# In the attention stage's tensor queue, three projection products stand ahead of each turn of the probabilities instead of behind it

## The chip, the cores and the metric

The kernel runs on one core of a Trainium2 chip. TensorE (PE) multiplies; VectorE (DVE) and ScalarE (ACT) read its result banks in PSUM; GpSimd (POOL) adds the mask; SyncE (SP) issues the DMAs. The metric is the device time of one launch in microseconds (us).

## The reference

Inputs: x of 8 batches x 512 tokens x 512 features, a bias of 8 x 16 x 512 x 512 numbers (134 MB), a mask, and the weights of two layers. Cut to what matters:

```
# layer 0: per batch either a dense net (gelu) or a small circuit, then a norm
x = layernorm(where(vol > 0.5, x + circuit(x), x + gelu(x@w1+b1)@w2+b2))
# layer 1
x = layernorm(x)*(1+scale) + shift
q, k, v = x@Wq+bq, x@Wk+bk, x@Wv+bv              # 16 heads of 32
scores = q@k.T/sqrt(32) + attention_bias; scores[mask] = -inf
ctx = softmax(scores) @ v
x = x + ctx@Wo + bo
x = x + gelu2(layernorm(x)@W1 + b1) @ W2 + b2
```

## The kernel before

There are three stages one after the other: the first dense net (to about 793 us), attention (about 793 to 1673 us), the second dense net. Only the order of TensorE's work in the attention stage is touched.

Attention goes batch by batch (8 of them, `b`), and a batch has 16 **slots** `m` (4 head groups x 4 blocks of 128 queries). A slot handles 4 **units** (the 4 heads of a group for one query block, `j` = 0 to 3; their running number is n). Everything is written out by hand in program order on each engine; semaphores tie the engines together, and an engine never passes a waiting instruction of its own.

TensorE's slot `m`, in its order:

- `scores` (L1643): 12 matmuls for the *next* slot's four units, into four score banks. Waits on `scored`: DVE must have read the scores before.
- `context` (L1660): probabilities times v for the *previous* slot's units. It waits on `pt_even` and `pt_odd`, the counts of turned probabilities that ACT (units 0 and 2) and DVE (units 1 and 3) have copied out of PSUM.
- four **quarters** `j`. In each, `turn_unit` (L1672) transposes the unit's 128 x 512 exponentials by four transposes into bank `turn[j % 2]` (waits: `exped`, and the copy of the unit two before, since it reuses its bank); and `beside` issues 3 of the 12 matmuls (L1587) of one 128 x 512 product. A slot has one such product, all twelve matmuls into one bank, `gen`: slots 0 to 3 the output projection of the batch before (`OUTS`), slots 4 to 7, 10, 11, 14, 15 a key or query projection (`KEYS`; the last four for the next batch), slots 8, 9, 12, 13 the next batch's values (`VALUES`). The last batch has none in slots 8 to 15; the first has one in slot 0 and none in 1 to 3.
- after a fourth slot, `over` (L1630): 4 transposes of the inverse sums. After slots 5 and 6, two `turn_x` (L1597): 4 transposes each of the next batch's input, into the banks `turn[0]` and `turn[1]`, each after the copy out of the unit that was there (`pt_even`, `pt_odd`).

Before the first product matmul of a slot, `gen_free` makes TensorE wait until the bank `gen` was emptied of the product of the slot before. After a slot of `KEYS` that takes two steps: `nat_hi_of` on ACT (L1299), then `nat_lo_of` on DVE (L1440), which raises `nat_lo`.

ACT's slot: [`over`, L1324, at phase starts], emptying of `gen` where it is ACT's (L1299, L1305), then copy of unit 0 (L1318), `exp` of the next slot's units 0 and 1 (L1311), [`context_hi`, L1330, at phase starts], copy of unit 2, `exp` of units 2 and 3.

DVE's slot: its emptying of `gen` (L1440, or L1446 after `OUTS`), bias addition and maximum of the next slot's units 0 and 1 (L1452), [`normalize`, L1473, at phase starts; `inverse` at phase ends], copy of unit 1 (L1459), L1452 of units 2 and 3, [`context_lo`, L1477, at phase starts], copy of unit 3, [mask conversion, L1431].

In slot 0 the last 3 matmuls of the output projection also wait on `ct_lo`, which `context_lo` raises:

```
            if i == 0 and steps[-1] == 3 * KT - 1:
                pe.wait_ge(ct_lo, b * PHASES + PHASES)
```

Of the kernel before, what the change touches and what calls it, by code (L numbers as in the profile page):

```python
# [1086 lines left out]
def attention_stage(nc, ctx, mem, banks, small, keep, t, scratch, ffn0, ffn1):  # L1087
# [61 lines left out]
    def following(b, m, last):  # L1149

        if m + 1 < BLOCKS:
            return b, m + 1
        return None if last else (b + 1, 0)
# [425 lines left out]
    def tensor(pe, f0, f1):  # L1579
# [10 lines left out]
        def turn_x(b, k, bank, last=False):  # L1590
            if k == 0 and last:
                pe.wait_ge(s1["affine_done"], TT)
            elif k == 0:
                pe.wait_ge(x_in, b * 32 + 16)
            for i in range(TT):
                tile = xin8[:, i, :] if last else xin[i // 2][:, i % 2, :]
                mm = pe.transpose(bank[:, i * P:(i + 1) * P], tile[:, k * P:(k + 1) * P], keep.ident[:, :])  # L1597
            mm.then_inc(x_mm, 1)

        def project(odd, tile, query, steps, bank):  # L1600
            wh, wl = weight["q" if query else "k"]
            cut = slice(tile * P, (tile + 1) * P)
            mm = part(bank[:, :], steps, lambda k: (wh[:, k, cut], wl[:, k, cut], xth[odd][:, k, :], xtl[odd][:, k, :]))
            if steps[-1] == 3 * KT - 1:
                mm.then_inc(nat_mm, 1)

        def values(odd, i, steps, bank):
            wh, wl = weight["v"]
            cut = slice(i * P, (i + 1) * P)
            mm = part(bank[:, :], steps, lambda k: (xth[odd][:, k, cut], xtl[odd][:, k, cut], wh[:, k, :], wl[:, k, :]))  # L1610
            if steps[-1] == 3 * KT - 1:
                mm.then_inc(v_mm, 1)

        def output(b, i, steps, bank):
            if i == 0 and steps[0] == 0:
                pe.wait_ge(w_lo, 4)
                pe.wait_ge(ct_lo, b * PHASES + PHASES - 1)
            if i == 0 and steps[-1] == 3 * KT - 1:
                pe.wait_ge(ct_lo, b * PHASES + PHASES)
            wh, wl = weight["o"]  # L1620
            cut = slice(i * P, (i + 1) * P)
            mm = part(bank[:, :], steps, lambda k: (cth[:, k, cut], ctl[:, k, cut], wh[:, k, :], wl[:, k, :]))
            if steps[-1] == 3 * KT - 1:
                mm.then_inc(o_mm, 1)

        def over(b, phase):
            pe.wait_ge(spread_set, b * PHASES + phase + 1)
            pe.wait_ge(pt_even, b * (UNITS // 2) + 2 * (TT * phase + TT))
            for u in range(TT):
                mm = pe.transpose(turn[0][:, u * P:(u + 1) * P], normal[:, u * P:(u + 1) * P], keep.ident[:, :])  # L1630
            mm.then_inc(over_mm, 1)

        def scores(b, m, first=False):

            tile, u = divmod(m, TT)
            if u == 0:
                pe.wait_ge(nat_lo, nat_count(b, tile, 1))
            if m or not first:
                pe.wait_ge(scored, b * UNITS + GROUP * m)
            for q, k in ((QH, KH), (QL, KH), (QH, KL)):  # L1640
                for j in range(GROUP):
                    head = nat[tile % 2][j * HD:(j + 1) * HD, :, :]
                    mm = pe.matmul(score[j][:, :], head[:, q, u * P:(u + 1) * P], head[:, k, :],  # L1643
                                   start=(q, k) == (QH, KH), stop=k == KL)
                    if k == KL:
                        mm.then_inc(score_mm, 1)

        def context(b, odd, m, first):

            tile, u = divmod(m, TT)  # L1650
            pe.wait_ge(pt_even, b * (UNITS // 2) + 2 * m + 2)
            pe.wait_ge(pt_odd, b * (UNITS // 2) + 2 * m + 2)
            if m == 0:
                pe.wait_ge(v_out, b * TT + TT)
            if u == 0 and not (first and m == 0):
                pe.wait_ge(normed, b * PHASES + tile)
            for k in range(KT):
                for j in range(GROUP):
                    h = GROUP * tile + j
                    mm = pe.matmul(ctx_ps[j * HD:(j + 1) * HD, u * P:(u + 1) * P], v[odd][:, k, h * HD:(h + 1) * HD],  # L1660
                                   pt[:, j, k, :], start=k == 0, stop=k == KT - 1)
            mm.then_inc(pv_mm, 1)

        def turn_unit(b, m, j, first):
            n = GROUP * m + j
            pe.wait_ge(exped, b * UNITS + n + 1)
            if not first or n >= 2:
                pe.wait_ge(pt_odd if n % 2 else pt_even, b * (UNITS // 2) + n // 2)
            if j == 0 and m % TT == 0 and not (first and m == 0):
                pe.wait_ge(over_out, b * PHASES + m // TT)  # L1670
            for k in range(KT):
                mm = pe.transpose(turn[n % 2][:, k * P:(k + 1) * P], bias[:, n % SLOTS, k * P:(k + 1) * P], keep.ident[:, :])  # L1672
            mm.then_inc(turned, 1)

        def gen_free(b, m, first):

            if m in OUTS and m and not first:
                pe.wait_ge(o_out, b * TT - TT + OUTS[m])
            elif m in OUTS or (m == 4 and first):
                pe.wait_ge(nat_lo, nat_count(b, 1, 0 if m == 0 and first else 1))  # L1680
            elif m == 4:
                pe.wait_ge(o_out, b * TT)
            elif m == 8:
                pe.wait_ge(nat_lo, nat_count(b, 3, 1))
            elif m in (9, 13):
                pe.wait_ge(v_out, b * TT + TT + VALUES[m])
            elif m in (10, 14):
                pe.wait_ge(v_out, b * TT + TT + VALUES[m - 1] + 1)
            elif m == 12:
                pe.wait_ge(nat_lo, nat_count(b + 1, 0, 1))  # L1690
            else:
                tile, query = KEYS[m]
                pe.wait_ge(nat_lo, nat_count(b, tile, query) - 1)

        def beside(b, odd, m, j, first, last):
            some = range(3 * j, 3 * j + 3)
            keys = FIRST_KEYS if first else KEYS
            if m in keys and (keys[m][0] < KT or not last):
                if j == 0:
                    gen_free(b, m, first)  # L1700
                tile, query = keys[m]
                project(odd if tile < KT else 1 - odd, tile % KT, query, some, gen)
            elif m in VALUES and not last:
                if j == 0:
                    gen_free(b, m, first)
                values(1 - odd, VALUES[m], some, gen)
            elif m in OUTS and not first:
                if j == 0:
                    gen_free(b, m, first)
                output(b - 1, OUTS[m], some, gen)  # L1710
            elif m in LAST_TURNS and j == 1 and last:
                if LAST_TURNS[m] == 0:
                    pe.wait_ge(nat_lo, nat_count(b, 3, 1))
                else:
                    pe.wait_ge(xt_lo, x_count(b + 1) + LAST_TURNS[m])
                turn_x(b + 1, LAST_TURNS[m], gen, True)
# [19 lines left out]
        def body(b, odd, first, last):  # L1736
            for m in range(BLOCKS):
                after = following(b, m, last)
                if after:
                    scores(*after)  # L1740
                if m:
                    context(b, odd, m - 1, first)
                elif not first:
                    context(b - 1, 1 - odd, BLOCKS - 1, False)
                for j in range(GROUP):
                    for k in TURNS.get(m - 1, ()):
                        if j == k % 2 and not last:
                            pe.wait_ge(xt_lo, x_count(b + 1) + k + 1)
                    turn_unit(b, m, j, first)
                    beside(b, odd, m, j, first, last)  # L1750
                if m % TT == TT - 1:
                    over(b, m // TT)
                for k in TURNS.get(m, ()):
                    if not last:
                        pe.wait_ge(pt_odd if k % 2 else pt_even, b * (UNITS // 2) + 2 * m + 2)
                        turn_x(b + 1, k, turn[k % 2])
# [151 lines left out]
```

## Time and profile before

| | |
|---|---|
| median of 3 runs | 2397.74 us (2396.6 to 2398.53) |
| the profiled execution's own time | 2398.12 us |
| its span, first to last instruction | 2396.3 us |
| TensorE busy | 2362.5 us (99%) |
| DVE, ACT, POOL busy | 57%, 42%, 43% |
| mean granted TensorE clock | 0.998 of full |

The span is the length of the profiled execution; the time of a run has a further 1.8 us around it. TensorE's busy time is that of pipelined matmuls, so what a slot costs is read from the starts of its instructions and not from their lengths. The attention stage is 37% of the span.

### The profile page before, as it was taken

To read this page: it belongs to the slowest core of one execution; us is meant where nothing else is said; L and a number is where in the kernel's file an instruction comes from. 1 tells how busy PE (TensorE), PEld (TensorE's weight loads), DVE (VectorE), ACT (ScalarE), POOL (GpSimd) and SP (SyncE) were. 2 spreads that over 40 slices of the span, in tenths; PEclk is the share of its full clock that TensorE was granted. 3 is DMA by queue.
4 is the path that set the end of the run, shared out by engine and by line. 5 is a ranking of instruction groups with operands and counts; after the bars stand their busy time and mean duration, and the time that the engine had idled before them with its cause. 6 is when DMAs were issued, how large, how long until landed. Compare 5 with 4: busy or idle time off the path is not lost. (4 is left out here: it accounts for less than half of the span.)

```text
span 2396.3 us, 42236 instructions
## 1 busy us (share of the span) xinstructions
PE 2362.5 (99%) x16100; PEld 1894.6 (79%) x16100; DVE 1359.5 (57%) x2749; ACT 1012.1 (42%) x2057; POOL 1019.7 (43%) x829
## 2 busy tenths in 40 slices
PE   9999999999999899999999999997999999999999
PEld 7788888888888677777777777775888888888887
DVE  7355464555557777777777777778443333323332
ACT  6132232331332776776767676767311111111111
POOL 0042341432424896767677776767113203203200
PEclk9999999999999999999999999999999999999999
DMA  7110101101122556565656566564320110110100
GB/s 231 42 45 21 44 24 55 44 18 61 44 73 102 161 182 205 168 200 163 212 158 203 170 200 194 169 211 164 123 71 1 53 53 0 53 53 1 51 35 18
DMA packets 142197, 243.94 MB, mean 102 GB/s; under 512 B 14140, under 2 KB 28620, under 8 KB 142048
## 3 DMA queue, kind: packets, MB, share of 16 engines
q1 hardware_dynamic: 141520, 241.66, 31.4%
q8 instruction: 97, 1.59, 0.3%
q14 instruction: 52, 0.43, 0.1%
q10 hardware_dynamic: 528, 0.26, 0.0%
HBM read 216.69 MB, written 25.20 MB: 101 GB/s over the span
## 5 line engine op out<-in xcount | busy, mean ns | idle before, releaser
L1254 POOL TENSOR_TENSOR at_bias<-at_bias,at_mask 128x512 f32<-128x512 f32 x512 | 596.4, 1192 | 231.7 <-DMA at_bias<-in_fside_Bx16xSxS 224.8
L646 ACT ACTIVATE L_hid<-bank,L_b1c 128x512 f32<-128x512 f32 x256 | 176.6, 690 | 962.0 <-PE bank L290 961.8
L845 DVE CAST L_hh<-L_hid 128x512 fp32r<-128x512 f32 x256 | 122.9, 480 | 739.1 <-PE bank L972 710.5
L288 PE MATMUL bank<-xth,L_w1h 128*128 128x512 f32 x1024 | 403.2, 394 | 0.1
L289 PE MATMUL bank<-xth,L_w1l 128*128 128x512 f32 x1024 | 400.0, 391 | 0.0
L290 PE MATMUL bank<-xtl,L_w1h 128*128 128x512 f32 x1024 | 399.7, 390 | 0.0
L970 PE MATMUL bank<-L_w2h,L_hh 128*128 128x512 f32 x1016 | 398.4, 392 | 0.0
L972 PE MATMUL bank<-L_w2l,L_hh 128*128 128x512 f32 x1016 | 396.0, 390 | 0.0
L971 PE MATMUL bank<-L_w2h,L_hl 128*128 128x512 f32 x1016 | 395.8, 390 | 0.0
L1311 ACT ACTIVATE at_bias<-at_bias,cos_sin 128x512 f32<-128x512 f32 x512 | 363.3, 713 | 8.5 <-DVE cos_sin L1452 8.0
L1452 DVE CUSTOM_DVE_ANT_0 at_bias<-bank,at_bias 128x512 f32<-128x512 f32 x512 | 331.3, 684 | 36.6 <-PE bank L1643 24.6
L541 POOL TENSOR_TENSOR rstd<-mv,power 128x4 f32<-128x4 f32 x24 | 25.8, 1077 | 730.1 <-DVE mv L729 730.0
L1672 PE MATMUL bank<-ident,at_bias 128*128 128x128 f32 x2048 | 313.9, 277 | 8.3 <-DVE at_pt L1459 5.5
L1672 PEld LDWEIGHTS bank<-ident,at_bias 128*128 128x128 f32 x2048 | 243.5, 141 | 84.6 <-issue 33.9
L1318 ACT ACTIVATE at_pt<-bank 128x512 f32<-128x512 f32 x256 | 152.3, 595 | 233.8 <-PE bank L1672 233.8
L847 DVE TENSOR_TENSOR L_hl<-L_hid,L_hh 128x512 fp32r<-128x512 f32 x256 | 232.4, 908 | 8.8
L1459 DVE COPY at_pt<-bank 128x512 f32<-128x512 f32 x256 | 176.0, 688 | 96.6 <-PE bank L1672 96.1
L288 PEld LDWEIGHTS bank<-xth,L_w1h 128*128 128x128 f32 x1024 | 192.6, 188 | 48.2 <-issue 8.2
L290 PEld LDWEIGHTS bank<-xtl,L_w1h 128*128 128x128 f32 x1024 | 192.7, 188 | 41.1
L289 PEld LDWEIGHTS bank<-xth,L_w1l 128*128 128x128 f32 x1024 | 192.7, 188 | 39.4
L972 PEld LDWEIGHTS bank<-L_w2l,L_hh 128*128 128x128 f32 x1016 | 190.8, 188 | 39.9
L970 PEld LDWEIGHTS bank<-L_w2h,L_hh 128*128 128x128 f32 x1016 | 190.9, 188 | 38.8
(213 smaller groups left out, 3240.9 us busy)
## 6 DMA issues: line engine op xcount, KB each, us to landing
at_bias<-in_fside_Bx16xSxS SPq DMA_DIRECT2D x256, 512.0 KB, 3.7
L_xres<-in_x SPq DMA_DIRECT2D x8, 1024.0 KB, 5.3
x_scratch<-L_xres SPq DMA_DIRECT2D x8, 1024.0 KB, 4.3
at_xres<-x_scratch SPq DMA_DIRECT2D x32, 256.0 KB, 4.3
L_xin<-x_scratch SPq DMA_DIRECT2D x8, 1024.0 KB, 5.6
L_xres<-x_scratch SPq DMA_DIRECT2D x8, 1024.0 KB, 5.6
L_ring<-in_L_cond_w SPq DMA_DIRECT2D x31, 256.0 KB, 4.9
L_xin<-in_x SPq DMA_DIRECT2D x7, 1024.0 KB, 5.2
```

Source lines behind the costliest of these rows:

```text
L288: nc_mm = pe.matmul(out, ah, bh, start=i == 0, stop=False)
L289: nc_mm = pe.matmul(out, al, bh, start=False, stop=False)
L290: nc_mm = pe.matmul(out, ah, bl, start=False, stop=i == n - 1)
L646: nc.scalar.activation(hid[m % 2][:, :], turn[m % 2][:, :], func, bias=b1c[:, m:m + 1]).then_inc(h_act, 1)
L847: nc.vector.tensor_tensor(hl[m % 2][:, :], hid[m % 2][:, :], hh[m % 2][:, :].bitcast(F32), ALU.subtract)\
L970: pe.matmul(acc[i][:, :], hh[m % 2][:, cut], w2h[:, m, :], start=m == 0, stop=False)
L971: pe.matmul(acc[i][:, :], hl[m % 2][:, cut], w2h[:, m, :], start=False, stop=False)
L972: mm = pe.matmul(acc[i][:, :], hh[m % 2][:, cut], w2l[:, m, :], start=False, stop=m == FT - 1)
L1254: nc.gpsimd.tensor_tensor(tile, tile, mask[:, m % TT, :], ALU.add).then_inc(masked, 1)
L1311: nc.scalar.activation(tile, tile, ACT.Exp, bias=neg_top[:, n % SLOTS:n % SLOTS + 1], scale=-1.0, accum_out=sums[:, n:n + 1]).then_inc(exp ...
L1452: nc.vector.tensor_tensor_reduce(bias[:, slot, :], score[j][:, :], bias[:, slot, :], -1.0, -MASKED, ALU.add, ALU.min, neg_top[:, slot:slot ...
L1672: mm = pe.transpose(turn[n % 2][:, k * P:(k + 1) * P], bias[:, n % SLOTS, k * P:(k + 1) * P], keep.ident[:, :])
```

## The change

In each quarter the call of `beside` is put ahead of the turn, and ahead of the wait on `xt_lo` that goes with it. Nothing is added or removed.

```
                 for j in range(GROUP):
+                    beside(b, odd, m, j, first, last)
                     for k in TURNS.get(m - 1, ()):
                         if j == k % 2 and not last:
                             pe.wait_ge(xt_lo, x_count(b + 1) + k + 1)
                     turn_unit(b, m, j, first)
-                    beside(b, odd, m, j, first, last)
```

The orders of DVE, ACT, POOL and SP are the same as before. What moves on TensorE is shown at three places of one middle batch. The first is TensorE at the head of slot 5 (the scores of slot 6's units, the context of slot 4's, then slot 5's first quarter), in the order before:

```order
L1643 MATMUL bank<-at_nat 128x512 x11
L1660 MATMUL bank<-at_pt,at_v 32x128 [waits at_normed,at_pt_odd,at_pt_even]
L1660 MATMUL bank<-at_pt,at_v 32x128 x15
L1672 MATMUL bank<-ident,at_bias 128x128 [waits at_pt_even,at_exped]
L1672 MATMUL bank<-ident,at_bias 128x128 x3
L1587 MATMUL bank<-xth,at_wqh 128x512 [waits at_nat_lo]
L1587 MATMUL bank<-xth,at_wql 128x512
L1587 MATMUL bank<-xtl,at_wqh 128x512
```

and of the change:

```order
L1643 MATMUL bank<-at_nat 128x512 x11
L1660 MATMUL bank<-at_pt,at_v 32x128 [waits at_normed,at_pt_odd,at_pt_even]
L1660 MATMUL bank<-at_pt,at_v 32x128 x15
L1587 MATMUL bank<-xth,at_wqh 128x512 [waits at_nat_lo]
L1587 MATMUL bank<-xth,at_wql 128x512
L1587 MATMUL bank<-xtl,at_wqh 128x512
L1672 MATMUL bank<-ident,at_bias 128x128 [waits at_pt_even,at_exped]
L1672 MATMUL bank<-ident,at_bias 128x128 x3
```

The wait on `nat_lo`, the emptied `gen`, now stands right behind the context. The second place is TensorE at the end of slot 5, before:

```order
L1672 MATMUL bank<-ident,at_bias 128x128 [waits at_pt_odd,at_exped]
L1672 MATMUL bank<-ident,at_bias 128x128 x3
L1587 MATMUL bank<-xth,at_wqh 128x512
L1587 MATMUL bank<-xth,at_wql 128x512
L1587 MATMUL bank<-xtl,at_wqh 128x512
L1597 MATMUL bank<-ident,at_xin 128x128 [waits at_x_in,at_pt_even]
L1597 MATMUL bank<-ident,at_xin 128x128 x3
L1597 MATMUL bank<-ident,at_xin 128x128 [waits at_pt_odd]
```

and of the change:

```order
L1587 MATMUL bank<-xth,at_wqh 128x512
L1587 MATMUL bank<-xth,at_wql 128x512
L1587 MATMUL bank<-xtl,at_wqh 128x512
L1672 MATMUL bank<-ident,at_bias 128x128 [waits at_pt_odd,at_exped]
L1672 MATMUL bank<-ident,at_bias 128x128 x3
L1597 MATMUL bank<-ident,at_xin 128x128 [waits at_x_in,at_pt_even]
L1597 MATMUL bank<-ident,at_xin 128x128 x3
L1597 MATMUL bank<-ident,at_xin 128x128 [waits at_pt_odd]
```

The last turn of the slot is now next to the transposes of the input, which reuse its bank. The third place is TensorE at the end of slot 0, before:

```order
L1672 MATMUL bank<-ident,at_bias 128x128 [waits at_pt_odd,at_exped]
L1672 MATMUL bank<-ident,at_bias 128x128 x3
L1587 MATMUL bank<-at_woh,at_cth 128x512 [waits at_ct_lo]
L1587 MATMUL bank<-at_woh,at_ctl 128x512
L1587 MATMUL bank<-at_wol,at_cth 128x512
L1643 MATMUL bank<-at_nat 128x512 [waits at_scored]
L1643 MATMUL bank<-at_nat 128x512 x11
```

and of the change:

```order
L1587 MATMUL bank<-at_woh,at_cth 128x512 [waits at_ct_lo]
L1587 MATMUL bank<-at_woh,at_ctl 128x512
L1587 MATMUL bank<-at_wol,at_cth 128x512
L1672 MATMUL bank<-ident,at_bias 128x128 [waits at_pt_odd,at_exped]
L1672 MATMUL bank<-ident,at_bias 128x128 x3
L1643 MATMUL bank<-at_nat 128x512 [waits at_scored]
L1643 MATMUL bank<-at_nat 128x512 x11
```

The wait on `ct_lo` now stands ahead of the last turn.

## Rows read from the trace of the kernel before

**Rows 1.** Stretches: length, busy PE, PEld, DVE, ACT, POOL, clock, DMA share, GB/s.

```profile
793.20:906.50 113.30, 105.60 (x1143) 80.44 (x1142) 91.39 (x213) 86.21 (x201) 98.59 (x83) 1.00 0.57 175
906.50:1566.00 659.50, 654.96 (x7105) 508.60 (x7104) 505.61 (x1176) 464.00 (x1104) 472.24 (x408) 1.00 0.59 185
...
1620.00:1630.00 10.00, 7.01 (x95) 4.94 (x97) 7.87 (x19) 8.25 (x19) 7.91 (x7) 0.91 0.65 217
```

**Rows 2.** Waits of PE, 899 to 1560 us: total us, times, longest.

```profile
PE bank L1587 <- DVE at_ctl L1477: 3.4, 6, 0.8
```

**Rows 3.** Timeline of PE, slot 14 of batch 3: start, length, instruction.

```profile
1222.44 0.97 PE L1643 MATMUL bank<-at_nat 32*128 32x512 f32 x12
1223.35 1.08 PE L1660 MATMUL bank<-at_pt,at_v 128*32 128x128 f32 x32
1224.36 0.66 PE L1672 MATMUL bank<-ident,at_bias 128*128 128x128 f32 x4
...
1225.54 0.60 PE L1672 MATMUL bank<-ident,at_bias 128*128 128x128 f32 x4
...
1226.67 0.60 PE L1672 MATMUL bank<-ident,at_bias 128*128 128x128 f32 x4
...
1227.79 0.60 PE L1672 MATMUL bank<-ident,at_bias 128*128 128x128 f32 x4
...
1229.02 0.97 PE L1643 MATMUL bank<-at_nat 32*128 32x512 f32 x12
```

**Rows 4.** Timeline of ACT in the same slot.

```profile
1227.30 0.60 ACT L1318 ACTIVATE at_pt<-bank 128x512 f32<-128x512 f32 x1 [0.25 <-PE bank L1672]
1227.80 0.71 ACT L1311 ACTIVATE at_bias<-at_bias,cos_sin 128x512 f32<-128x512 f32 x1
...
1229.21 0.67 ACT L1299 ACTIVATE at_nat<-bank,at_biases 128x512 fp32r<-128x512 f32 x1
```

**Rows 5.** Timeline of DVE in the same slot.

```profile
1226.17 0.69 DVE L1459 COPY at_pt<-bank 128x512 f32<-128x512 f32 x1 [1.27 <-PE bank L1672]
...
1228.43 0.69 DVE L1459 COPY at_pt<-bank 128x512 f32<-128x512 f32 x1 [0.34 <-PE bank L1672]
...
1229.91 0.75 DVE L1440 SCALAR_TENSOR_TENSOR at_nat<-bank,at_biases,at_nat 128x512 fp32r<-128x512 f32 x1 [0.46 <-ACT at_nat L1299]
```

**Rows 6.** Timeline of DVE, then of PE: a first product that waited for `gen`.

```profile
798.74 0.75 DVE L1440 SCALAR_TENSOR_TENSOR at_nat<-bank,at_biases,at_nat 128x512 fp32r<-128x512 f32 x1 [1.87 <-ACT at_nat L1299]
...
799.55 0.50 PE L1587 MATMUL bank<-xth,at_wqh 128*128 128x512 f32 x1 [0.96 <-DVE at_nat L1440]
```

**Rows 7.** Timeline of PE: matmuls 128x512 right behind the last context.

```profile
1672.87 0.50 PE L288 MATMUL bank<-xth,L_w1h 128*128 128x512 f32 x1
1673.20 0.40 PE L289 MATMUL bank<-xth,L_w1l 128*128 128x512 f32 x1
```

**Rows 8.** Timeline of PE, end of slot 5 of batch 4: two `turn_x`.

```profile
1276.57 1.03 PE L1597 MATMUL bank<-ident,at_xin 128*128 128x128 f32 x8
1277.54 0.98 PE L1643 MATMUL bank<-at_nat 32*128 32x512 f32 x12
```

**Rows 9.** Timeline of DVE, then of PE: slot 0 of batch 4.

```profile
1239.84 0.68 DVE L1459 COPY at_pt<-bank 128x512 f32<-128x512 f32 x1
...
1241.65 0.74 DVE L1477 SCALAR_TENSOR_TENSOR at_ctl<-at_normal,at_biases,at_cth 128x512 fp32r<-128x512 f32 x1
...
1241.38 0.60 PE L1672 MATMUL bank<-ident,at_bias 128*128 128x128 f32 x4
1242.45 0.50 PE L1587 MATMUL bank<-at_woh,at_cth 128*128 128x512 f32 x1 [0.47 <-DVE at_ctl L1477]
```

**Rows 10.** Timeline of DVE, then of PE: a turn that waited for a copy.

```profile
1289.95 0.68 DVE L1459 COPY at_pt<-bank 128x512 f32<-128x512 f32 x1
...
1290.78 0.63 PE L1672 MATMUL bank<-ident,at_bias 128*128 128x128 f32 x4 [0.24 <-DVE at_pt L1459]
```

**Rows 11.** Timeline of DVE, slot 12 of batch 3.

```profile
1214.57 1.50 DVE L1477 SCALAR_TENSOR_TENSOR at_ctl<-at_normal,at_biases,at_cth 128x512 fp32r<-128x512 f32 x1
```

More of the change, by code:

```diff
@@ L1745, in body @@
                 for j in range(GROUP):
+                    beside(b, odd, m, j, first, last)
                     for k in TURNS.get(m - 1, ()):
@@ L1749, in body @@
                     turn_unit(b, m, j, first)
-                    beside(b, odd, m, j, first, last)
                 if m % TT == TT - 1:
```

## The prediction

> **What bounds the kernel now.** The stretches of the trace come first. In the six middle batches of attention TensorE is busy for 654.96 of 659.50 us at full clock, and DVE, ACT and POOL each for 464 to 506 us [rows 1]: TensorE sets the pace, and a batch (109.9 us) is the sum of what it issues. Its waits there are few, mainly six on `ct_lo` in slot 0 for 3.4 us [rows 2]. So the change can win almost nothing from waits. The question is which waits it makes. For that I read one slot on three engines, by starts.
>
> TensorE, slot 14 of batch 3 [rows 3]: scores at 1222.44, context 0.91 later, first turn T0 1.01 after that, T1 1.18 later, T2 and T3 each 1.13 later, next scores at 1229.02: a slot is 6.58 us. ACT in that slot [rows 4]: its copy of unit 2 starts 0.63 after T2 starts, waits end with T2; then it is busy without a gap: copy 0.50, two `exp` in 1.41, and `nat_hi` starts at 1229.21, 1.91 after the copy. DVE starts `nat_lo` 0.70 later, at 1229.91 [rows 5]. From the start of `nat_lo` to a first product that waits for it are 0.81 us [rows 6]. So **`gen` is free 0.63 + 1.91 + 0.70 + 0.81 = 4.05 us after T2 starts**. This chain is set by T2, not by the product's end, since the emptying of `gen` stands behind ACT's copy of unit 2 and two `exp`.
>
> **The change, part by part.** The matmuls are the same; only places move.
>
> (a) Issue cost. Before, a product's three matmuls follow transposes or lead into the scores. Afterwards the slot's first three stand right behind the context. Matmuls of this size right behind a context take 0.33 from the first to the second [rows 7]. A further one takes 0.23 (a quarter of 1.13 less four transposes of 0.109, by three), so 0.80 us from product to T0. The other quarters keep 1.13 us. A turn that leads into scores instead of a product: eight transposes to the scores took 0.97 us [rows 8]; at 0.109 each (within a turn) four take 0.53. New slot without waits: 0.91 + 1.01 + 0.80 + 3 x 1.13 + 0.53 = 6.64 against 6.58. I take +0.055 a slot, 0.9 us a batch. The Trainium skill (TensorE: Matmul & The Clock Gate, Back-to-back issue gap) gives 512/2.4 + 2.5 = 216 ns for such a matmul; three in 0.65 instead of 0.80 us would turn this term into a gain of 0.10 a slot. The row shows the dearer start behind a context [rows 7], and I go by it; from it and from 0.69 us (three at 0.23) the bounds are +0.9 and -0.9 us a batch.
>
> (b) **The emptying of `gen`.** Before, the first product had until after T0: from T2, 1.13 + 1.23 (T3 to scores) + 0.91 + 1.01 + 0.4 (T0) = 4.68 us, against 4.05 needed: covered, 0.6 to spare. Afterwards each turn stands a product later, right ahead of the scores, and the next product stands ahead of T0. From T2 to that product: 1.13 + 0.53 + 0.91 + 1.01 = 3.58 us. The chain still needs 4.05. TensorE waits 0.47 us, and everything behind it with it, T2 of that slot too, so nothing is caught up in the next slot. At phase starts ACT has `context_hi` between (it delays the copy of unit 2), at phase ends the transposes of the sums and their ACT copy; these add about as much to the chain as to TensorE's time, and I take 0.48 everywhere. It applies where the slot before held a `KEYS` product: slots 5, 8, 11, 12, 15 and 0, six a batch. Slots 6 and 7 follow the input's transposes (0.87 us more of cover) and are free. After values or output products one engine empties `gen` (ACT straight behind its last `exp`, or DVE behind the copy of unit 3, both about 2.1 after T3, and 2.45 are there): free. 6 x 0.48 = 2.9 us a batch. Bounds: 0 if the chain is shorter than I read, 0.69 each (the whole shift of the turn) if nothing covers: 0 to 4.1.
>
> (c) **Slot 0, `ct_lo`.** DVE's copy of unit 1 starts 1.81 before `context_lo` [rows 9], and 0.80 after its start the product goes on. Before, DVE could take that copy at 1239.84 without waiting for TensorE; the product waited to 1242.45, where T3 at 1241.38 + 0.36 (three steps of 0.109 and a little) would have let it: 0.71 us, of which the trace counts 0.47 as idle. The six such waits together are 3.4 [rows 2], 0.57 each, so about 0.81 by this count. Afterwards T1 starts 0.80 + 1.13 behind the slot's first product, the copy 0.63 later, and the product goes on at 2.56 + 1.81 + 0.80 = 5.17; TensorE is there at 0.80 + 2.26 + 0.36 = 3.42. Wait 1.75 instead of 0.81: +0.9 us a batch. This holds only if DVE's copy is paced by T1; if not, 0.
>
> (d) **Slots 5 and 6, `turn_x`.** The second `turn_x` needs the copy of unit 3. A turn that waits for a copy starts 0.83 after it [rows 10], and the copy starts 0.63 to 0.64 after T3 starts [rows 3, 5]: 1.46 behind T3. Before, a product (0.8) and a `turn_x` (0.44) stood between; now only the `turn_x`, so TensorE is there at 0.88. Wait 0.58, twice: 1.2 us a batch.
>
> (e) **The context.** It needs the same copy, 1.46 behind T3; TensorE is there at 0.53 + 0.90 = 1.43. 0.03 in plain slots. At phase starts DVE has three operations and `context_lo` after the copy of unit 1 (2.49 us, where T1 to T3 are 2.26), so 0.26 each in slots 4, 8, 12. In slot 12 `context_lo` is stretched by POOL's work in some batches, to 1.50 [rows 11]; I take another 0.5. Together 1.5; part of slot 12's was there before, so 1.35 us a batch.
>
> (f) Bias loads. SP's loads wait on T1 and T3, which are up to 0.8 us later in their slot; they are for the slot four further, some 26 us. Nothing.
>
> **Sum.** 0.9 + 2.9 + 0.9 + 1.2 + 1.35 = 7.25 us a middle batch, six of them: 43.5. The first batch has no slot-0 term but the others and waits longer for `gen` in slot 5: 6. The last has only eight slots with products, slots 6 and 7 without `turn_x` (0.6 each), and four late transposes ahead of T1 on a chain that TensorE waits for: 5. In all +54 us on a span of 2396.3, with 1.8 around it 2452; the profiled run was 0.4 above the median, so **2451 us**.
>
> **The rivals.**
>
> *The waits of (b) don't come* (the chain behind T2 is overtaken, say because ACT's queue is shorter than in my slot): 21 us of the 54 fall away, 2430. For it: my slot is one of many [rows 4, 5]. Against it: each step in them is one operation after another without a gap. With (c) halved too, 2427.
>
> *Only the issue cost*: all waits covered, +6 us, 2404. That needs `nat_lo` to start by 2.77 after T2, and the slot has 3.24 [rows 3, 5].
>
> *Not slower.* The place is the first product behind the context. If it starts as behind a transpose (three in 0.69 us), a slot is 6.53 us, 0.05 less, over 117 slots 6 us faster: 2392. It decides if at the same time `gen` is free 3.58 after T2; the rows have 4.05, and with six waits a batch above 0.02 us each the gain is already gone. Little speaks for it.
>
> *The clock falls.* In the last batch, where slots hold turns and waits without products, the mean granted clock was 0.91 of full over 1620 to 1630 us [rows 1]: it had gone from 2.4 to 1.2 GHz for part of it. Slot 0 gets a wait of 1.75 us between products. If that drops the clock there for some 7 us, TensorE loses about 3.5 us in each of seven batches: 24 more, 2475. Against it: in the first batch TensorE idled 7.7 of 113.3 us and the clock stayed at 1.00, 2.4 GHz [rows 1], and products surround the new waits. The Trainium skill (TensorE: Matmul & The Clock Gate, The HAM clock gate) has the clock gate close after sustained idleness, and says that transposes don't count as busy; by that rule turns around a wait could add up, and no row here shows it with products between.
>
> **How the numbers follow.** My forecast 0.62; (b) absent or halved 0.16; the clock, or DVE's delays adding up, 0.13; only the issue cost 0.04; not slower 0.05. The likeliest case's own range is 2435 to 2466. To leave out no more than 2 in 10 the range reaches to the second and the third: 2424 to 2472. Differences under 0.2% (4.8 us) can't be told from no change in this kernel. Faster 0.03, same 0.03, slower 0.94 (the issue cost alone is just over the bound).
>
> **What the changed profile would show.** Waits of PE at L1587 on DVE's `at_nat` about 36 times at near 0.45 us, none before; the wait on `at_ctl` at 1.5 or more in slot 0; `turn_x` (L1597) waiting on L1459 about 14 times at 0.5; a first product 0.80 ahead of T0; a middle batch of 117 us. Waits on `at_nat` missing would refute (b), a second product less than 0.3 behind the first after a context (a). The prediction is wrong if DVE or ACT reach their work in another order of lateness than this one slot shows, or if the clock moves.

## The result, and the profile after

The changed kernel takes **2456.14 us** (median of 4 runs, 2452.05 to 2458.79) against 2397.56 (4 runs beside it, 2396.6 to 2398.53): 1.0244 of the time before [1.0232, 1.0256], 58.6 us slower. 2451 was forecast. The profiled execution took 2457.95, its span is 2456.1.

The stretches of the same parts of attention come first (first batch, six middle batches, last batch; columns as in [rows 1]):

```profile
794.10:915.39 121.29, 108.48 (x1141) 82.67 (x1140) 90.44 (x213) 85.18 (x200) 97.32 (x83) 0.99 0.52 162
915.39:1616.11 700.72, 669.19 (x7107) 519.00 (x7106) 498.35 (x1177) 459.37 (x1105) 471.16 (x408) 1.00 0.55 175
1616.11:1732.90 116.79, 97.41 (x1110) 74.72 (x1110) 86.60 (x201) 78.15 (x184) 78.29 (x65) 0.94 0.55 176
```

The middle batches took 659.5 us before [rows 1] and take 700.7: 41.2 more, 6.9 a batch, with the same matmuls and a mean granted clock that rounds to 1.00. One batch of the six holds a short fall of the clock that costs 1.5 us (below); without it the waits and the new order cost 6.6 a batch. The first batch is 8.0 us longer (121.29 against 113.30), the last 9.8 by the starts of its slots (116.4 against 106.6). With the 0.9 us by which attention starts later that makes 59.9, and the spans differ by 59.8. The second dense net takes 723.2 us as before (723.4).

The waits of PE in the middle batches (total us, times, longest) answer to [rows 2], where the six on `at_ctl` were nearly all (3.4 of 4.3 us):

```profile
PE bank L1587 <- DVE at_nat L1440: 14.2, 34, 0.5
PE bank L1587 <- DVE at_ctl L1477: 9.3, 6, 1.6
PE bank L1597 <- DVE at_pt L1459: 4.2, 12, 0.3
PE bank L1660 <- issue: 2.8, 11, 0.6
```

These are the four kinds that the prediction names: `gen` (b), `ct_lo` (c), the second `turn_x` (d), the context (e). Those for `gen` and `turn_x` were not there before; the context's were 0.7 us, 2 times.

**The emptying of `gen`.** Slot 14 of batch 3 and the start of slot 15, first PE, then ACT, then DVE (answers to [rows 3 to 5]):

```profile
1255.74 0.60 PE L1672 MATMUL bank<-ident,at_bias 128*128 128x128 f32 x4
...
1257.40 0.97 PE L1643 MATMUL bank<-at_nat 32*128 32x512 f32 x12
1258.35 1.08 PE L1660 MATMUL bank<-at_pt,at_v 128*32 128x128 f32 x32
1259.80 0.50 PE L1587 MATMUL bank<-xth,at_wqh 128*128 128x512 f32 x1 [0.36 <-DVE at_nat L1440]
1256.38 0.60 ACT L1318 ACTIVATE at_pt<-bank 128x512 f32<-128x512 f32 x1 [0.27 <-PE bank L1672]
...
1258.28 0.67 ACT L1299 ACTIVATE at_nat<-bank,at_biases 128x512 fp32r<-128x512 f32 x1
1258.99 0.75 DVE L1440 SCALAR_TENSOR_TENSOR at_nat<-bank,at_biases,at_nat 128x512 fp32r<-128x512 f32 x1 [0.45 <-ACT at_nat L1299]
```

T2 starts at 1255.74. ACT's copy follows 0.64 later, `nat_hi` 1.90 after that, `nat_lo` 0.71 after that, the first product 0.81 after that: 4.06 us from T2, forecast 4.05. TensorE would have been there 1.01 after the context, at 1259.36. It waits 0.44.

**`ct_lo`.** Slot 0 of batch 4, DVE and then PE (answers to [rows 9]):

```profile
1269.98 0.69 DVE L1459 COPY at_pt<-bank 128x512 f32<-128x512 f32 x1 [0.80 <-PE bank L1672]
...
1271.81 0.75 DVE L1477 SCALAR_TENSOR_TENSOR at_ctl<-at_normal,at_biases,at_cth 128x512 fp32r<-128x512 f32 x1
1269.35 0.60 PE L1672 MATMUL bank<-ident,at_bias 128*128 128x128 f32 x4
...
1270.47 0.60 PE L1672 MATMUL bank<-ident,at_bias 128*128 128x128 f32 x4
1272.61 0.50 PE L1587 MATMUL bank<-at_woh,at_cth 128*128 128x512 f32 x1 [1.54 <-DVE at_ctl L1477]
```

DVE's copy of unit 1, without a wait in [rows 9], now waits 0.80 us for T1, and the product stands 3.26 us behind T1. Without the wait it would start at 1270.47 + 0.36: it waits 1.78, where 1.75 was forecast.

**`turn_x`.** The end of slot 6 of batch 4, PE and then DVE (answers to [rows 8], which are the same place in slot 5):

```profile
1315.86 0.60 PE L1672 MATMUL bank<-ident,at_bias 128*128 128x128 f32 x4
1316.30 0.60 PE L1597 MATMUL bank<-ident,at_xin 128*128 128x128 f32 x4
1317.24 0.66 PE L1597 MATMUL bank<-ident,at_xin 128*128 128x128 f32 x4 [0.35 <-DVE at_pt L1459]
1316.49 0.69 DVE L1459 COPY at_pt<-bank 128x512 f32<-128x512 f32 x1 [0.35 <-PE bank L1672]
```

The eight transposes that ran as one group in [rows 8] are two groups with a wait between. The second starts 1.38 behind T3; two steps of 0.44 would have it there at 0.88. It waits 0.5.

To see all sixteen slots I took the starts of PE's groups from the two traces (mean of the six middle batches, us; "context at" and "product at" count from the slot's scores; a slot with a plain context and no wait has them at 0.90 and 1.91):

```
slot            15    0    1    2    3    4    5    6    7    8    9   10   11   12   13   14   sum
longer by     0.54 1.55 0.31 0.11 0.11 0.04 1.36 0.60 -.06 0.57 0.28 0.12 0.54 0.58 0.12 0.12  6.9
context at    0.94 0.90 0.98 0.94 0.94 0.90 1.30 0.90 0.90 0.90 1.12 0.94 0.94 0.91 1.12 0.95
product at    2.39 2.44 2.13 1.96 1.96 1.91 2.65 1.91 1.91 2.44 2.13 1.96 2.39 2.45 2.13 1.96
```

Slot 1's figures are not those of a typical batch. In five of the six its context starts at 0.90, its product at 1.91 and it is 0.06 longer; in batch 5, where the clock fell, they are 1.37, 3.23 and 1.57.

### The profile page after: what moved, and what is told of

Same layout as the page of the kernel before. It is cut to its first block and busy times, and to the rows that moved or that the text cites. A ratio compares the mean times of both kernels' runs of the same rounds, so it can differ in the third digit from the quotient of the medians.

```text
span 2456.1 us, 42236 instructions
## 1 busy us (share of the span) xinstructions
PE 2382.8 (97%) x16100; PEld 1909.7 (78%) x16100; DVE 1348.7 (55%) x2749; ACT 1006.2 (41%) x2057; POOL 1017.5 (41%) x829
## 3 DMA queue, kind: packets, MB, share of 16 engines
q8 instruction: 97, 1.59, 0.3%
## 5 line engine op out<-in xcount | busy, mean ns | idle before, releaser
L1672 PE MATMUL bank<-ident,at_bias 128*128 128x128 f32 x2048 | 308.5, 274 | 8.6 <-DVE at_pt L1459 5.7
L1672 PEld LDWEIGHTS bank<-ident,at_bias 128*128 128x128 f32 x2048 | 254.6, 142 | 77.8 <-issue 7.6
L290 PEld LDWEIGHTS bank<-xtl,L_w1h 128*128 128x128 f32 x1024 | 192.5, 188 | 41.2
```

Of the source, the lines that this page charges most:

```text
L290: nc_mm = pe.matmul(out, ah, bl, start=False, stop=i == n - 1)
```

## The experiments

All edits but two are made to the changed kernel. Runs 1 to 4 change which quarters, or which slots, have the product ahead; runs 5 to 8 leave TensorE's order and move what makes it wait; 9 and 10 do both. The waits listed are those of PE in the six middle batches of the run's own trace.

**1. Quarter 0 as before** (the product behind T0, quarters 1 to 3 changed).

```
                 for j in range(GROUP):
-                    beside(b, odd, m, j, first, last)
+                    product_first = j > 0
+                    if product_first:
+                        beside(b, odd, m, j, first, last)
...
                     turn_unit(b, m, j, first)
+                    if not product_first:
+                        beside(b, odd, m, j, first, last)
```

> The changed kernel (2456 us) with quarter 0 alone back in the old order: turn, then three products; quarters 1 to 3 keep products first. My theory: what quarter 0 did was to bring the first product, and with it the wait for the emptied bank gen, a turn (0.44 us) closer to the context, and to leave the dearer start behind the context to a product. Both go: from T2 to the first product are then 3.58 + 0.41 = 3.99 us against 4.05 needed, so the waits on at_nat in the six slots of a middle batch shrink from 0.46 to under 0.1 us. The waits on at_ctl in slot 0 (1.5), of turn_x (0.35 idle by the trace) and of the context stay. Forecast 2428 us (2420 to 2434). Rival, that the cost is TensorE's lateness in all quarters whatever stands first: only a quarter of the 58 us goes, 2442. Rival, that it is all in the issue of products behind transposes: no more than 6 us go, 2450.

Measured: 2431.87 us, 1.0142 [1.0126, 1.0157], 24.3 less than the changed kernel. Waits of PE in its middle batches:

```profile
PE bank L1587 <- DVE at_ctl L1477: 9.9, 6, 2.2
PE bank L1660 <- issue: 5.6, 13, 1.1
...
PE bank L1587 <- DVE at_nat L1440: 0.3, 2, 0.2
```

The `gen` waits fall from 14.2 to 0.3 us. Those for `ct_lo` stay, but for one slot where `context_lo` took 1.46 us instead of 0.75. Those of the context double, and they do so in slot 13, where it starts at 1.61 instead of 1.12: `context_lo` in the slot before took 1.02 to 1.72 us in the six batches, where it took 0.75 in each of the changed kernel. With other waits gone, it runs at another time against the other engines.

**2. Quarter 0 alone changed** (as 1, with `product_first = j == 0`).

> The other half of e1: only quarter 0 has its products first, quarters 1 to 3 turn first as before. T1 now follows T0 at once, so T2 and T3 keep their old distance to the scores and only T0 is a product later. My theory: from T2 to the first product are 1.13 + 1.23 + 0.9 + 1.01 = 4.27 us; ACT, whose copy of unit 0 is late now, needs 4.39 in plain slots, 4.87 against 4.71 at phase ends, 5.0 against 4.27 after a phase start. That makes some 1.5 us a middle batch of waits on at_nat, with 0.9 for the dearer start behind the context, less 0.2 at at_ctl. No waits of turn_x or the context. Forecast 2414 us (2406 to 2422). Rival, that e1 and e9 share the loss as they share the quarters, three to one: 2412 as well, but with no waits on at_nat. Rival, that the two halves each cost what the whole costs less the other: 2456 - 2432 = 24 over before, 2421.

Measured: 2421.87 us, 1.0101 [1.0085, 1.0116], 24.3 above the kernel before. So quarter 0's product costs 24 us whether the other quarters are moved or not. Nine of its slots (2 to 4, 6, 7, 9, 10, 13, 14) have no new wait and are 0.04 to 0.06 us longer than before: that is the issue cost (a) by itself, forecast 0.055. Its largest `gen` wait is in slot 5, here in batch 3:

```profile
1171.93 1.08 PE L1660 MATMUL bank<-at_pt,at_v 128*32 128x128 f32 x32
1173.67 0.50 PE L1587 MATMUL bank<-at_xth,at_wqh 128*128 128x512 f32 x1 [0.66 <-DVE at_nat L1440]
1174.01 0.40 PE L1587 MATMUL bank<-at_xth,at_wql 128*128 128x512 f32 x1
```

The product starts 1.74 behind the context instead of 1.01: 0.73 us. From it to the second is 0.34.

**3. Quarter 3 as before** (`product_first = j < 3`).

> The changed kernel (2456 us) with quarter 3 alone back in the old order: T2, T3, then the last three products. My theory: the copy of unit 3 gets its product as cover again, so the waits of turn_x on L1459 (14 in the changed kernel) and those of the context (11 in the middle batches) go; the wait on at_ctl in slot 0 gets 0.44 us shorter, since T3 is issued ahead of it; the waits on at_nat behind the context stay, since T2 is as late as before. Forecast 2437 us (2430 to 2443). Rival, that these waits cost nothing because the wait on at_nat takes their place: 2452 or more.

Measured: 2442.9 us, 1.0189 [1.0173, 1.0204]. PE's waits in the middle batches:

```profile
PE bank L1587 <- DVE at_nat L1440: 13.8, 34, 0.5
PE bank L1587 <- DVE at_ctl L1477: 6.6, 6, 1.1
PE bank L1660 <- issue: 2.1, 7, 0.5
```

The waits of `turn_x` are gone and plain contexts start at 0.90 again: both come from T3 standing right ahead of them. The `gen` waits stay nearly as they were (13.8 against 14.2), as a chain that starts with T2 must have it; one that started with the copy of unit 3 would have become shorter.

**4. The change only in slots where nothing was expected to wait** (`product_first = m in (1, 2, 3, 9, 10, 13, 14)`).

> The new order only in slots 1, 2, 3, 9, 10, 13 and 14, the old one in all others. In these none of the waits of the changed kernel comes by my account, but for 0.03 us at the context. My theory: what is left is the issue cost of a product behind a context, 0.055 us a slot in 49 slots, with the context's 0.03: forecast 2401.5 us (2399 to 2404), 0.1 to 0.25% over before, and no new wait on at_nat over 0.1 us. Rival, that a product behind the context starts as fast as behind a transpose: 2395. Rival, that the change costs something in every slot: 7/16 of the 58 us, 2423.

Measured: 2407.38 us, 1.0038 [1.0025, 1.0052]; the forecast was 6 us too low. No wait on `at_nat` is left in the middle batches:

```profile
PE bank L1587 <- DVE at_ctl L1477: 3.3, 6, 1.0
PE bank L1660 <- issue: 1.9, 6, 0.3
PE bank L1672 <- DVE at_pt L1459: 1.6, 6, 0.4
```

A middle batch is 1.5 us longer than before. By its slots' starts, slots 2, 3, 10 and 14 are longer by 0.11 to 0.12, slots 1 and 9 by 0.06 to 0.07, slot 13 by 0.28; and two slots in the old order, which I had at nothing, by 0.55 together: slot 15 by 0.11, and slot 11 by 0.44, where T3 waits for DVE's copy of unit 1 (the third row). DVE in slot 11 of batch 1:

```profile
985.86 0.75 DVE L1440 SCALAR_TENSOR_TENSOR at_nat<-bank,at_biases,at_nat 128x512 fp32r<-128x512 f32 x1 [0.79 <-ACT at_nat L1299]
...
988.02 1.56 DVE L1468 COPY at_normal<-angle 128x512 f32<-128x512 f32 x1
989.51 0.68 DVE L1459 COPY at_pt<-bank 128x512 f32<-128x512 f32 x1
```

Slot 13's 0.28 is the issue cost and a context at 1.29 instead of 1.07: `context_lo` in slot 12 took 1.46 to 1.50 us in all six batches, where before it took 0.95 to 1.50.

In the rows of slot 11 there is no gap from `nat_lo` to the copy: the chain behind slot 10's T2 starts DVE's slot late, and the part of `inverse` that stands ahead of the copy takes 1.56 us. A slot's cost is partly paid in the one behind it.

**5. `nat_hi` one `exp` earlier.** ACT empties `gen` ahead of its slot's last `exp` instead of behind it.

```
-                if before in keys:
-                    tile, query = keys[before]
...
                 if after:
                     exp(*after, 2)
+                if m in keys:
+                    tile, query = keys[m]
+                    if tile < KT:
+                        nat_hi_of(b, tile, query, gen)
+                    elif not last:
+                        nat_hi_of(b + 1, tile - KT, query, gen)
+                if after:
                     exp(*after, 3)
```

> The changed kernel with TensorE's order untouched; on ACT the first step that empties gen after a key or query product (nat_hi, L1299) stands ahead of the last exp of its own slot instead of behind it. My theory: the chain behind T2 gets one exp (0.7 us) shorter, 3.4 us against 3.58 there are, so the waits of PE on at_nat go (45 of them, 23.6 us idle in the changed kernel) but for some after mask conversions, while the places of products and turns are as in the changed kernel. Forecast 2432 us (2426 to 2440). Rival, that the cost lies in TensorE's own order (weight loads, starts behind other kinds of work): the time stays at 2456. Rival, that DVE and not ACT is what is late: nat_lo still starts 3.2 us after T2 and the time stays.

Measured: 2439.46 us, 1.0176 [1.016, 1.0192], 16.7 less than the changed kernel, at the upper end of what was expected. ACT's order in its trace, and PE's waits in the middle batches (lines stand one further in this file):

```profile
1219.32 0.60 ACT L1318 ACTIVATE at_pt<-bank 128x512 f32<-128x512 f32 x1 [0.26 <-PE bank L1673]
...
1220.52 0.68 ACT L1299 ACTIVATE at_nat<-bank,at_biases 128x512 fp32r<-128x512 f32 x1
```
```profile
PE bank L1588 <- DVE at_ctl L1478: 9.4, 6, 1.7
PE bank L1661 <- issue: 4.9, 15, 1.1
...
PE bank L1588 <- DVE at_nat L1441: 0.3, 1, 0.3
```

`nat_hi` starts 1.20 behind the copy instead of 1.90, and the `gen` waits fall from 14.2 to 0.3 us with TensorE's order untouched: the cause of (b) is where the emptying stands on ACT. By the traces the middle batches gain 14.4 us, of which 1.5 are the fallen clock of batch 5, and not 6 x 2.8: the contexts wait 4.9 instead of 2.8 us, again mostly in slot 13 (`context_lo` 0.76 to 1.73 us in slot 12), and slots 6 and 7 have 0.13 each for `gen` (product at 2.04).

**6. `context_hi` and `context_lo` of slot 0 earlier**, behind ACT's copy of unit 0 and DVE's copy of unit 1.

```
                 turn_out(b, m, 0, first)
+                if m == 0 and not first:
+                    context_hi(b - 1, PHASES - 1)
...
-                elif u == 0 and not first:
-                    context_hi(b - 1, PHASES - 1)
...
                 turn_out(b, m, 1, first)
+                if m == 0 and not first:
+                    context_lo(b - 1, PHASES - 1)
...
-                elif u == 0 and not first:
-                    context_lo(b - 1, PHASES - 1)
```

> The changed kernel with TensorE's order untouched; in slot 0 alone ACT does context_hi right behind its copy of unit 0, ahead of two exp, and DVE does context_lo right behind its copy of unit 1, ahead of two score operations. My theory: the last product of slot 0 waits on ct_lo because context_lo stands 1.8 us behind a copy that T1 paces. Then it is 0.6 us behind that copy; the wait falls from about 1.75 to 0.55 us in seven batches. Forecast 2448 us (2444 to 2452), wait on at_ctl in the trace 7 times at 0.3 to 0.5 us idle instead of 1.5. Rival, that the wait is set by context_hi on ACT or by the normalisation: no change in it, 2456.

Measured: 2446.2 us, 1.0207 [1.0191, 1.0222]. In the middle batches the `ct_lo` waits are 3.2 us instead of 9.3 and those on `at_nat` 15.3; slot 0 takes 7.96 us instead of 8.98. The cause of (c) is shown too. The seven slots 0 give 6.7 us. Most of the rest by which this trace is shorter lies where the clock fell in the changed kernel's and not in this one (below).

**7. The same edit on the kernel before.** If (c)'s wait is the order's own, the kernel before has some 0.6 of it to win a batch.

> The kernel before, TensorE's order untouched, with the edit of ACT and DVE in slot 0 that took 10 us off the changed kernel: context_hi behind the copy of unit 0, context_lo behind the copy of unit 1. My theory: ct_lo then comes before TensorE needs it, the seven waits on at_ctl (3.8 us idle, 5.7 by the starts) go and nothing else starts to wait. Forecast 2392 us (2390 to 2395), ratio 0.9976. Rival, that the later score operations of units 2 and 3 make the next scores wait for as much: 2397, no change.

Measured: 2395.36 us, 0.9991 [0.9983, 1.0] (12 runs). PE's waits in its middle batches, then DVE and PE in slot 0 of batch 4 and behind it:

```profile
PE bank L1643 <- DVE cos_sin L1452: 1.5, 6, 0.3
...
PE bank L1587 <- DVE at_ctl L1477: 0.3, 1, 0.3
```
```profile
1240.90 1.27 DVE L1477 SCALAR_TENSOR_TENSOR at_ctl<-at_normal,at_biases,at_cth 128x512 fp32r<-128x512 f32 x1 [0.20 <-ACT at_cth L1330]
...
1243.45 0.51 PE L1643 MATMUL bank<-at_nat 32*128 32x512 f32 x4 [0.26 <-DVE cos_sin L1452]
```

The wait on `ct_lo` falls from 3.4 to 0.3 us, but `context_lo` now delays DVE's reading of units 2 and 3, and the next scores wait for that, 1.5 us. By the trace the middle batches are as long as before (110.0 against 109.9), and the interval reaches 1.0: no gain is shown, where 2392 was forecast.

**8. `context_lo` one step later**: as 7, but on DVE behind its reading of unit 2 instead of ahead of it.

> The kernel before with context_hi early as in e6, and context_lo one score operation later than there, between units 2 and 3. In e6 it ran beside POOL's mask addition and took 1.27 instead of 0.74 us, and the next scores waited 0.26 us in each batch. Here it starts 0.14 us later than TensorE needs for no wait, and only one score operation is late. My theory: wait on at_ctl 0.1 us, no wait of the scores, forecast 2393 us (2391 to 2397), ratio 0.998. Rival, that context_lo is stretched by POOL here too: then the wait on at_ctl is 0.6 us and the time that of before, 2397.

Measured: 2394.47 us, 0.9984 [0.9975, 0.9993] (11 runs), against 2398.45 beside it. No wait for the scores is left, 0.3 us on `ct_lo` and 1.2 for contexts; a middle batch is 0.4 us shorter. It is the fastest kernel of the case, by less than the 0.2% of the prediction; run 7 and run 8 can't be told apart.

**9. All three causes away**: quarter 3 as before, `nat_hi` as in 5, `context` as in 6.

> The changed kernel with all three repairs: nat_hi ahead of the last exp on ACT, context_hi and context_lo early in slot 0, and quarter 3 in the old order. Quarters 0 to 2 keep products first. If the waits on at_nat, at_ctl, of turn_x and of the context are the whole of the loss but for the start behind the context, what is left is 0.06 us a slot in some 115 slots, less the old waits on ct_lo: forecast 2402 us (2398 to 2407), and middle batches of 110.5 us. Rival, that something not in my list costs time: 2415 or more.

Measured: 2428.38 us, 1.0132 [1.0117, 1.0147], 26 above the forecast. The `gen` waits had come back elsewhere. PE's waits, then DVE and PE at the start of slot 7 of batch 3:

```profile
PE bank L1588 <- DVE at_nat L1441: 5.9, 12, 0.5
```
```profile
1189.77 0.69 DVE L1436 TENSOR_TENSOR xtl<-bank,xth 128x512 fp32r<-128x512 f32 x1 [1.72 <-ACT xth L1294]
1190.38 0.74 DVE L1441 SCALAR_TENSOR_TENSOR at_nat<-bank,at_biases,at_nat 128x512 fp32r<-128x512 f32 x1
1191.17 0.50 PE L1588 MATMUL bank<-at_xth,at_wqh 128*128 128x512 f32 x1 [0.50 <-DVE at_nat L1441]
```

After slots 5 and 6 ACT and DVE also take the turned input out of its banks, and on DVE `nat_lo` stands behind the first step of that (L1436), which waits for ACT's (L1294). The earlier `nat_hi` pushed ACT's L1294 back by its own length, to 2.48 us behind the copy of unit 2, so DVE waits 1.72 us, `nat_lo` came later and not earlier, and slots 6 and 7 wait 0.57 each for `gen` (product at 2.48 instead of 1.91), where the changed kernel has no wait. I had also counted the context's waits in slots 5, 9 and 13 at nothing; they add 1.15 a batch. The waits on `ct_lo` are 3.5 us and not gone: in its early place `context_lo` took 1.24 to 1.59 us in slot 0.

**10. The same, with `nat_hi` in its old place after slots 5 and 6.**

> As e7_all_three, but after slots 5 and 6 ACT keeps the old order of nat_hi. In e7 the early nat_hi pushed the last exp, the step of turn_x behind it and with it DVE's nat_lo back there, and the first products of slots 6 and 7 waited 0.57 us each that no other kernel has. If that is the mend's own cost, middle batches fall from 113.8 to 112.6 us and the kernel to 2420 us (2415 to 2424). If not, it stays at 2428.

Measured: 2419.8 us, 1.0086 [1.0071, 1.0102], as expected. The waits of PE in the middle batches:

```profile
PE bank L1664 <- issue: 9.4, 14, 1.1
PE bank L1591 <- DVE at_ctl L1481: 2.0, 4, 0.8
```

No wait on `at_nat` is left. A middle batch is 2.9 us longer than before, and 2.5 of it are the issue cost, 0.9, and the contexts, 9.4 / 6 = 1.6. They are those of slots 5, 9 and 13, right behind the slots with `context_lo`, which took 0.75 to 1.67 us in slot 4 and 0.96 to 1.74 in slot 12: about 1 us of the 2.9 is this stretch of one DVE instruction.

## Why the prediction held

Each step against the slots' starts in a middle batch, in us:

```
                            forecast   measured
(a) issue cost                 0.9       0.9    16 slots at 0.055; alone in run 2
(b) emptying of gen            2.9       2.8    6 waits of 0.34 to 0.54; away in runs 1 and 5
(c) ct_lo in slot 0            0.9       1.0    away in run 6
(d) second turn_x              1.2       1.1    2 waits of 0.55; away in run 3
(e) contexts                   1.35      0.9    partly away in run 3, largest in run 10
clock, batch 5 alone            -        0.25   1.5 us in one of six batches
sum                            7.25      6.9
```

- (a) The first product's second matmul starts 0.33 behind the first [rows 7], and the place behind the context is the dearer one. The rival "not slower" needed it to be the cheaper one and falls in run 2.
- (b) was read right from one slot: 4.06 for the chain, 3.6 for TensorE. "The waits don't come" and "only the issue cost" are refuted by 34 waits.
- (c) held, and so did its condition, that T1 paces DVE's copy: in [rows 9] it didn't, now it does.
- (e) was right where it rested on the queue of DVE (0.22 in slot 9, forecast 0.26). It was wrong in the half microsecond that I put on slot 13's context for a stretched `context_lo`: the context waits 0.17 there before and 0.22 after. The stretch itself is gone. In slot 12 `context_lo` took 0.95 to 1.50 us in the six middle batches before and 0.75 in each of them after; in slot 4 it took 0.75 to 0.95 before and 0.74 to 1.20 after, and slot 5's context waits 0.22 to 0.68, 0.40 on average, the more the longer it was. The step took a row of the old timing over into the new one.
- The **first batch** is the term that was mis-sized: 8.0 us where the prediction had 6. Slot 5 waits 2.4 us for `gen`, 1.3 at most before, and slot 6 0.96 more (product at 2.87 against 1.91). In the last batch slots 0 to 7 give 4.5 (59.4 against 54.9), with 1.4 us for `gen` in slot 6 where I had 0.6; slots 8 to 15 give 5.3, where I had about one, and most of that is the clock.
- That the total came so near is partly luck: the middle batches, without the clock, lost 39.7 us and not 43.5, and the first batch and the late start of attention (2.0 and 0.9 more) fill the gap.
- **The clock** I had as a rival with 24 us; it came in part. Slot 0 of batch 5 shows it, products on both sides of the wait:

```profile
1389.11 0.50 PE L1587 MATMUL bank<-at_woh,at_cth 128*128 128x512 f32 x1 [1.59 <-DVE at_ctl L1477]
...
1390.44 1.44 PE L1643 MATMUL bank<-at_nat 32*128 32x512 f32 x12
1391.81 1.93 PE L1660 MATMUL bank<-at_pt,at_v 128*32 128x128 f32 x32
```

The scores take 1.44 instead of 0.97 and the context 1.93 instead of 1.08: TensorE's granted clock went from 2.4 to 1.2 GHz and back (mean 0.88 over the stretch below), and the batch took 118.1 us where the other five took 116.4 to 116.6.

```profile
1385.00:1399.00 14.00, 12.41 (x104) 9.37 (x106) 8.06 (x20) 7.95 (x20) 6.85 (x6) 0.88 0.41 125
```

One of the seven waits of slot 0 did this, for 1.6 us, not the 3.5 in each that the rival had.

In the last batch's slots without products it costs more. Slots 14 and 15 of that batch, in the changed kernel and in that of run 6, which has the same order on TensorE throughout and on all engines there:

```profile
1715.60:1731.70 16.10, 13.04 (x123) 10.60 (x124) 9.56 (x21) 9.73 (x23) 2.23 (x2) 0.70 0.06 17
```
```profile
1705.90:1717.50 11.60, 8.71 (x120) 6.80 (x121) 9.41 (x21) 9.32 (x23) 3.33 (x3) 1.00 0.07 24
```

The granted clock is 0.70 in the one and 1.00 in the other, and the two slots take 16.1 us there and 11.7 here (11.1 before, at 1.00). So with the same order these 4.4 us needn't be there. With the 1.5 us of batch 5 some 5.9 of the 59.9 us go with the clock; what is left is 54, and the forecast, which had left the clock out, was 54.

All twelve traces say the same of these slots, which hold no product in any of them: slot 15 took 4.6 or 4.9 us in the seven traces where the clock stayed at 2.4 GHz, and 6.4 to 6.5 in the five where it fell; slot 14 took 6.5 to 6.7 in nine, and 8.5 to 9.6 in the three where it fell. The four runs of the changed kernel go the same way: 2452.05 and 2454.32 us at a mean clock of 0.997, 2457.95 at 0.995 and 2458.79 at 0.994. The clock falls there among turns that wait for copies. What decides whether it falls I didn't settle: no run changes the clock alone.

## What to carry to other kernels

An instruction that is moved ahead on a saturated engine earns nothing by itself; it gives up the cover of what it passes, and each wait tied to either of them must be recomputed from the place where its chain starts (here T2, not the product). Add up the chain on the other engines, including what they have queued ahead of the step that frees the buffer, and compare it with the time that the engine takes over the same stretch. Price edits together and not one by one: a chain that starts late can be paid for a slot later (slot 11 in run 4), an instruction that is moved ahead delays what stands behind it in its own queue (`nat_hi` in run 9), and work that keeps its place can come to run beside another engine's and take twice as long (`context_lo` in runs 1, 5 and 10). Runs 4 and 9 missed by 6 and 26 us for such effects.

## What the runs showed of the hardware

- A matmul of 128x512 that starts behind a context or a wait has the next 0.33 to 0.34 us behind it, in stream 0.23. Sixteen such starts a batch are 0.9 us.
- TensorE's granted clock can fall after a wait of 1.6 us with full-sized products on both sides (1.59 us idle in slot 0 of batch 5, mean 0.88 over the 14 us around it). Six such waits in the same trace did not bring it down, nor did the twelve in the middle batches of runs 1 and 5, of up to 2.2 us.
- DVE's `context_lo` took 0.74 us in one place [rows 9], 1.27 in run 7, and 1.50 in [rows 11], with operands of the same shape. In the twelve traces there are 384 of it: the 163 with no POOL instruction beside them took at most 0.753 us; all 182 that took more than 0.76 had POOL's mask addition beside them, and 39 that had POOL's work beside them took no longer. This goes together in every trace; no run moved POOL's work alone.
